# Straight-line attention code, eight input slots, and a packed last block in the feed-forward layers

## The reference

```python
h = _layernorm(x, axis=-1) * (1 + ca) + sa
x = x + ga * attn(h)        # 16 heads of 16; softmax over all 1024 keys
h = _layernorm(x, axis=-1) * (1 + cb) + sb
x = x + gb * ffn(h)         # two layers of the following
# one layer:
h = shift_token(x)          # the upper half of the columns comes from the token before
q, k, v = split(h @ wqkv)   # 8 heads of 64
q, k = rotary_xpos(l2norm(q) * qs, l2norm(k) * ksc)
x = x + local_attention(q, k, v) @ wo   # windows of 128 tokens, each with the window before it
h = layernorm(shift_token(x)) * lg + lb
a, g = split(h @ w1 + b1)   # 682 columns each
x = x + (a * gelu(g)) @ w2 + b2
```

## Time and profile before

| | us |
|---|---|
| median of three runs | 4847.93 |
| lowest, highest | 4840.43, 4849.11 |
| the profiled execution | 4837.09 |
| its span, first to last instruction | 4835.1 |

### The profile page before, as it was taken

How to read it: one execution, slowest core, us unless ns; L and a number is a source line. 1 busy time by engine, 2 the same in 40 slices (tenths; PEclk the granted TensorE clock), 3 DMA queues, 4 the chain that set the end, 5 groups by cost and what they waited for, 6 DMA issues and landing times. The chain is left out here.

```text
span 4835.1 us, 94881 instructions
## 1 busy us (share of the span) xinstructions
PE 4276.8 (88%) x27610; PEld 2744.2 (57%) x27610; DVE 3590.9 (74%) x7998; ACT 2801.1 (58%) x6209; POOL 1616.5 (33%) x2408
## 2 busy tenths in 40 slices
PE   5869999999999976599999997999799999988998
PEld 2423333333333334477777775888577777766787
DVE  6579888888888949688888784454688888875554
ACT  2438777777777850366666663333566666653333
POOL 2300000000000004455555553433455555545545
PEclk8969999999999998799999997999999999998999
DMA  6933323233233317200000002111100000012221
GB/s 204 367 54 61 60 42 60 46 57 54 48 61 50 52 63 243 72 25 26 24 24 26 24 23 63 44 54 35 49 24 25 25 24 25 25 30 85 68 65 51
DMA packets 368130, 297.05 MB, mean 61 GB/s; under 512 B 65820, under 2 KB 324888, under 8 KB 367648
## 3 DMA queue, kind: packets, MB, share of 16 engines
q1 hardware_dynamic: 367648, 291.11, 24.5%
HBM read 178.74 MB, written 111.21 MB: 60 GB/s over the span
## 5 line engine op out<-in xcount | busy, mean ns | idle before, releaser
L889 ACT ACTIVATE fa_P<-fa_pS 128x512 f32<-128x512 f32 x2048 | 1112.0, 595 | 385.7 <-PE fa_pS L815 337.6
L916 DVE TENSOR_REDUCE fa_mx<-fa_pR 128x2 f32<-128x1024 f32 x1024 | 1205.4, 1221 | 151.3 <-PE fa_pR L796 139.5
L1518 POOL TENSOR_TENSOR wa_pn<-wa_pr,wa_ri 128x512 f32<-128x512 f32 x512 | 700.7, 1369 | 614.0 <-DVE wa_ri L1574 600.4
L815 PE MATMUL fa_pS<-fa_Q,fa_K 50*128 50x512 f32 x2048 | 520.2, 504 | 108.0 <-ACT fa_P L889 77.8
L1454 ACT ACTIVATE wa_pr<-wa_sm,wa_mn 128x256 f32<-128x256 f32 x1024 | 510.4, 501 | 177.5 <-DVE wa_mn L1566 177.5
L1140 POOL TENSOR_TENSOR ao_xn<-ao_xn,ao_mod 128x1024 f32<-128x1024 f32 x16 | 37.6, 2348 | 1663.5 <-DVE ao_xn L1105 1663.5
L830 PE MATMUL fa_pO<-fa_P,fa_V 128*32 128x512 f32 x4096 | 560.1, 620 | 0.2 <-ACT fa_P L889 0.2
L815 PEld LDWEIGHTS fa_pS<-fa_Q,fa_K 50*128 50x128 f32 x2048 | 194.6, 187 | 602.9 <-ACT fa_P L889 543.4
L796 PE MATMUL fa_pR<-fa_K,fa_Q 48*128 48x512 f32 x2048 | 406.8, 451 | 60.6 <-DMA fa_K<-parts_d 38.5
L1306 PE MATMUL wa_pQK<-wa_wqkv,wa_xT 128*128 128x512 f32 x1536 | 419.7, 409 | 5.8 <-DVE wa_qa L1611 5.8
L2012 ACT ACTIVATE ff_gl<-ff_pG,ff_b 128x512 f32<-128x512 f32 x192 | 132.6, 691 | 475.2 <-PE ff_pG L1953 475.2
(11 more groups left out here) (186 smaller groups left out, 7191.8 us busy)
## 6 DMA issues: line engine op xcount, KB each, us to landing
parts_d<-pj_parts SPq DMA_DIRECT2D x64, 512.0 KB, 5.4
fa_Q<-parts_d SPq DMA_DIRECT2D x192, 128.0 KB, 4.5
fa_K<-parts_d SPq DMA_DIRECT2D x192, 128.0 KB, 6.9
v_d<-pj_v SPq DMA_DIRECT2D x16, 1024.0 KB, 8.4
fa_V<-v_d SPq DMA_DIRECT2D x32, 512.0 KB, 8.8
pj_x<-in_L_attn_x SPq DMA_DIRECT2D x16, 512.0 KB, 7.6
fa_Q<-fa_nrow SPq DMA_DIRECT2D x512, 2.0 KB
att_d<-fa_att SPq DMA_DIRECT2D x64, 128.0 KB, 2.0
```

The source lines that it names most:

```text
L815: nc.tensor.matmul(pS[:, (s * exped.per + u + e) % T, :], Ks[at:at + SROWS + 2, s, a, kb * P:(kb + 1) * P], Qs[at:at + SROWS + 2, s, a, ha ...
L889: nc.scalar.activation(Pr[:, k % 2, h, :], pS[:, (s * exped.per + u) % T, :], ACT.Exp).then_inc(exped.sem, 1)
L916: nc.vector.tensor_reduce(mx[:, q // QB, :, a, q % QB, kh], row_slot(), AX.X, ALU.max).then_inc(row_free, 1)
L1518: nc.gpsimd.tensor_tensor(pn[:, hp % 2], pr[:, hp % 2], inv, ALU.mult).then_inc(s["weighted"].sem, 1)
```

## The change

Four things are changed. Both `drive` functions of the attentions lose their loops: all 32 groups and all 67 bodies of a layer are written out on every engine, so that group and tile numbers, and the counts that waits compare with, are constants. The tiles xs and xo in local attention have eight slots (`X_BUFS`) in place of four, and SyncE loads tile n+8 after the store of tile n; the other tiles with `WIN_BUFS` slots stay at four. In feed-forward, the two halves of block 5 are packed into one block of 128 rows: the 42 value columns at rows 0 to 41, the 42 gate columns at rows 64 to 105. `up` then has eleven groups of six matmuls a tile and not twelve; gelu 5 reads rows 64 to 127 of pG, mix 5 and the splits of block 5 work on 64 rows, and mix 5 reads pG. The weights of block 5 come by one more DMA, and the unused rows of u are zeroed once. The normalization of the next tile is cut into three portions in place of five: steps 0 to 5 after mix 0, 6 to 11 after mix 1, 12 and hn after mix 2.

```diff
 WIN_BUFS = 4
+X_BUFS = NW
...
         def drive(eng, body):
-            body(0, 0)
-            loops = (GROUPS - NB) // NB
-            with eng.Fori(0, loops) as i:
-                for j in range(NB):
-                    body(i * NB + 1 + j, (1 + j) % NB)
-            for n in range(1 + loops * NB, GROUPS):
+            for n in range(GROUPS):
                 body(n, n % NB)
...
-        xs = sb("xs", [P, R, 2, P])
-        xo = sb("xo", [P, R, P])
+        xs = sb("xs", [P, X_BUFS, 2, P])
+        xo = sb("xo", [P, X_BUFS, P])
...
         def drive(eng, body):
-            for i in range(NW):
-                body(i, i)
-            with eng.Fori(1, B) as b:
-                for w in range(NW):
-                    body(b * NW + w, w)
-            for i in range(TILES, TILES + 3):
+            for i in range(TILES + 3):
                 body(i, i % NW)
...
-                for n in range(1, R):
+                for n in range(1, X_BUFS):
                     load(n, n)
-                with sp.Fori(0, TILES // R - 1) as i:
-                    for r in range(R):
-                        store(i * R + r, r % 2)
-                        load(i * R + R + r, r)
-                for n in range(TILES - R, TILES):
+                for n in range(TILES):
                     store(n, n % 2)
+                    if within(n + X_BUFS):
+                        load(n + X_BUFS, n % X_BUFS)
...
                     if within(new):
-                        turn_x(new, w % R)
+                        turn_x(new, w)
...
                     if within(end):
-                        add(end, w_end % R)
+                        add(end, w_end)
...
-        gated=HB, lifted=HB, gelu=HB, mixed=HB, u_high=HB, u_split=HB, y_done=1, summed=1, scaled=1, final=1,
+        gated=HB, lifted=HB - 1, gelu=HB, mixed=HB, u_high=HB, u_split=HB, y_done=1, summed=1, scaled=1, final=1,
...
+                w1_rows = a["L0_ffn_w1"][layer].rearrange("(k p) n -> p k n", p=P)
+                loads += [
+                    (w1_in[:, :, 0, 0:HID], w1_rows[:, :, 0:HID]),
+                    (w1_in[:, :, 1, 0:full], w1_rows[:, :, HID:HID + full]),
+                    (w1_in[:, :, 0, full + LAST:full + LAST + HL], w1_rows[:, :, HID + full:2 * HID]),
+                ]
...
+                nc.vector.memset(u[LAST:P, :, HB - 1, :].bitcast(F32), 0.0).then_inc(zeroed, 1)
...
                 def mix(n, j):
+
                     dve.wait_ge(s["gelu"].sem, s["gelu"].upto(g(n), j + 1))
-                    dve.wait_ge(s["lifted"].sem, s["lifted"].upto(g(n), j + 1))
+                    if j < HB - 1:
+                        dve.wait_ge(s["lifted"].sem, s["lifted"].upto(g(n), j + 1))
                     if not (early(n, 1) and layer == 0 and j < 2):
                         dve.wait_ge(s["u_split"].sem, g(n) * HB + j - 1)
-                    nc.vector.scalar_tensor_tensor(out=uF[:, j % 2, :], in0=pA[:, j % 2, :], scalar=b1[:, 0, j:j + 1],
-                                                   in1=gl[:, j % 2, :], op0=ALU.add,
-                                                   op1=ALU.mult).then_inc(s["mixed"].sem, 1)
+                    rows_, ps = (P, pA) if j < HB - 1 else (LAST, pG)
+                    nc.vector.scalar_tensor_tensor(out=uF[0:rows_, j % 2, :], in0=ps[0:rows_, j % 2, :],
+                                                   scalar=b1[0:rows_, 0, j:j + 1], in1=gl[0:rows_, j % 2, :],
+                                                   op0=ALU.add, op1=ALU.mult).then_inc(s["mixed"].sem, 1)
...
-                NORM_PARTS = (range(0, 1), range(1, 4), range(4, 8), range(8, 12), range(12, LN_INCS + 1))
+                NORM_PARTS = (range(0, 6), range(6, 12), range(12, LN_INCS + 1))
...
                 pe.wait_ge(w_in, 16 * LOADS)
+                pe.wait_ge(zeroed, 4)
...
                     for j in range(HB):
                         for half, ps, done, freed in ((1, pG, "gated", "gelu"), (0, pA, "lifted", "mixed")):
+                            if half == 0 and j == HB - 1:
+                                continue
                             if not (early(n, 1) and layer == 0 and j < 2):
                                 pe.wait_ge(s[freed].sem, g(n) * HB + j - 1)
+                            if half == 1 and j == 1 and not (early(n, 1) and layer == 0):
+                                pe.wait_ge(s["mixed"].sem, s["mixed"].upto(g(n - 1)))
+                            part = half if j < HB - 1 else 0
                             products = [(k, x, y) for k in range(KT) for x, y in SPLIT_PRODUCTS]
                             for i, (k, x, y) in enumerate(products):
-                                last = nc.tensor.matmul(ps[:, j % 2, :], w1[:, x, k, half, j * P:(j + 1) * P],
+                                last = nc.tensor.matmul(ps[:, j % 2, :], w1[:, x, k, part, j * P:(j + 1) * P],
...
-                    nc.scalar.activation(gl[:, j % 2, :], pG[:, j % 2, :], ACT.Gelu,
-                                         bias=b1[:, 1, j:j + 1]).then_inc(s["gelu"].sem, 1)
+                    at, rows_ = (0, P) if j < HB - 1 else (LAST, LAST)
+                    nc.scalar.activation(gl[0:rows_, j % 2, :], pG[at:at + rows_, j % 2, :], ACT.Gelu,
+                                         bias=b1[at:at + rows_, 1, j:j + 1]).then_inc(s["gelu"].sem, 1)
```

More of the change, by code:

```diff
@@ L1740, in feed_forward @@
         full = (HB - 1) * P
-        LOADS = 11
+        LOADS = 12
+        LAST = P // 2
         def g(n):
```

19 lines of the change are left out of this document (9 added, 10 removed).

## The result

| | before, us | after, us |
|---|---|---|
| median of four runs each | 4848.52 | 4623.24 |
| lowest, highest | 4840.43, 4865.0 | 4615.12, 4625.81 |
| the profiled execution's span | 4835.1 | 4613.0 |

The ratio is 0.953, with a 95% interval from 0.950 to 0.956: 225 us less. The forecast was 4626.

What follows compares the result with a forecast made beforehand. TensorE was taken as the bound, busy 1371 of 1507 us in full attention. Terms 75 + 83 + 22.4 + 35 = 215 us off 4837.1 gave 4622, 4633 with the median's 10.8; 4626 was taken, range 4595 to 4665.

Steps and rivals of the forecast that it cites:

- Full attention, 75 forecast: Full attention written out: 63 half groups at 21.67 us each take 1365 us instead of 1439.8; bounds 20 to 75.
- The 29 us of 54 halves: Full attention: 54 half groups in the loop each lose 0.54 us, with register instructions standing between the matmuls.
- The rest, the round ends: Full attention: the remainder of the 75 us is the eight loop-round ends with their slow clock.
- Local attention, 83 forecast: Local attention written out with eight slots: all tiles at 13.64 us, saving 41.8 and 40.8 us; bounds 12 to 83.
- with eight it has four bodies more, so the input waits go whatever else happens: Local attention: eight slots give each load some 55 us more, removing input waits of 6.0 us in layer 0.
- Where the instructions come from: Whole kernel: straight code's instruction fetch stays hidden, as in a written-out stretch with 5 packets; cost 0.
- The second rival: Straight code starved of instructions: 2.5 us for each of 243 packets, 608 us, time about 5230; chance 0.04.
- Feed-forward of layer 0, 22.4 forecast: Feed-forward, layer 0: one matmul group less, 1.40 us for each of 16 tiles, as TensorE never pauses; bounds 0 to 22.4.
- 3.0 us of cover: Feed-forward, layer 0: time between `split_h` ending and the next tile's matmuls; the later chain takes about 0.8 us of it.
- Feed-forward of layer 1, 35 forecast: Feed-forward, layer 1: packing and an earlier hn save 2.2 us a tile over 16 tiles; bounds 0 to 44.7.
- three steps held before mix 1: Feed-forward, layer 1: GpSimd holds small VectorE steps, mix 1 ends about 4581.6, block 3's value matmuls lose 0.6 us.
- the first rival: Feed-forward, layer 1: GpSimd always goes first, block 3 loses 1.7 us, the layer gains only 8; time 4653, chance 0.13.

Runs made afterwards that it cites:

- that experiment: Eight input slots alone against the kernel before, all loops kept: 4828.9 us, local attention 889.0 and 889.7 us a layer, no wait for an input.

## Why the prediction was right, and where it was not

**Full attention, 75 forecast, 77.3 measured: right, in size and cause.** The 29 us of 54 halves are there, but they are ScalarE's register instructions. The forecast said only that "register instructions stand between the matmuls", which put them on the wrong engine. The rest, the round ends, belongs to two engines: TensorE alone straight saves 17.2 us, ScalarE alone 38.4, both 73.9. Both together save more than the two savings add up to, since each engine's pause at a round end hides the other's.

**Local attention, 83 forecast, 92 measured: right in sum, wrong in one attribution.** The step "with eight it has four bodies more, so the input waits go whatever else happens" is true of the slots, as that experiment shows; but the forecast took it for the reason. Straight code takes them too, with four slots, where SyncE issues the load 1.1 us sooner. Of the 9 us more than forecast, 6 are tiles of 13.59 us in place of 13.64 (2 x 63 x 0.05). The other 3 come from the last two tiles of layer 1, which took 23.6 us before as well and which the forecast had counted as full tiles. With straight code, four slots and eight are alike. I had read a wait of at most 1.1 us as a matter of distance in tiles, and not looked at what SyncE does between the addition and the load.

**Where the instructions come from: right.** 193 packets, no pause for issue on TensorE in full attention (445 to 1650 us) and none over 0.3 us in local attention. The second rival needed 0.9 us a packet. The Trainium skill (Runtime: NRT & Kernel Launch, "Instruction fetch mechanics") says that a taken branch whose target lies outside the prefetched instructions forces a fetch, while straight code streams. The traces agree: waits of up to 3.8 us at the ends of long rounds, and none over 0.3 us in straight code.

**Feed-forward of layer 0, 22.4 forecast, 23.6 measured: right in size, wrong in reason.** The step that fails is "TensorE has no pause in this stage, so 22.4 us go, if nothing else is late". I looked for what becomes late at the tile's end and gave it 3.0 us of cover; hn, ready just in time before the transposes, I credited to layer 1 alone. By the packing alone the layer gains 1.7 us in all. The three portions, which I had put at nothing in this layer, make the gain possible, and give 0.17 us a tile of their own. The forecast counted 16 tiles and the distances are 15: 15 x 1.40 = 21.0, and 2.6 of the portions, are the 23.6. (One row less stands ahead of the transposes than before, the six value matmuls of block 5, and not two as the remark above the order of instructions says.)

**Feed-forward of layer 1, 35 forecast, 27.4 measured: the mechanism is right, the term too large.** The wait moved from hn to mix 1 as described. The forecast had three steps held before mix 1 and 0.6 us lost at block 3; four were held and 1.39 lost, nearer to the first rival's 1.7 than to 0.6. The fourth is L86, whose two inputs both lie in SBUF. The Trainium skill (SBUF — State Buffer, "Who interferes with whom") says that this form contends with GpSimd's reads, and the rows at 4403.52 and 4395.04 agree: 1.19 and 1.14 us behind the start of a GpSimd operation, 0.16 without. Its rule of the lock gave 8 us for a VectorE that loses every race, and that didn't happen: held steps and GpSimd's operations took turns, one for one. That the additions of GpSimd are the cause is shown: with them behind the splits, the wait and 22 us are gone. A part of the 27.4 is luck: the kernel before had two falls of the clock in this stage and the changed one none. Against unchanged code without a fall (417.0 us, in the kernel with TensorE's code straight) the gain is 24.1.

**The range** of 4595 to 4665 held the result. The errors of the terms were +2.3, +9.0, +1.2 and -7.6 us; they cancel in part, to +4.9, and the hit of the sum, 3 us, is better than its terms deserve.

## What to carry to other kernels

- Where an engine loop's round is long, write it out or shorten the round, and do so on every engine of the pipeline at once: in full attention each engine's pause at the round end hid the other's, and one engine's straight code gave a quarter (TensorE) or a half (ScalarE) of the gain of both.
- Less work on the busiest engine is worth nothing if its next operand is only just in time. Read the time between the operand's end and its use in the timeline before you credit the saving, and move the producer with it.
- Before a transfer is given more buffers, look at what its issuing engine does between the event that frees the buffer and the issue. And put GpSimd operations that nobody waits for behind those that somebody waits for, since each of them can also hold a small VectorE step.

## What the runs showed of the hardware

- A round end cost TensorE 2.5 us on the mean in full attention (20.1 / 8) and 3.6 in local attention (21.4 / 6), ScalarE 1.8 and 2.5 (14.1 / 8, 14.8 / 6), and TensorE 1.6 and 2.0 with six feed-forward tiles a round. With two such tiles a round there was none.
- After most pauses of TensorE at round ends in the attentions the granted clock went to 1.2 GHz for 3.4 to 13.7 us, but after those in feed-forward it didn't. In feed-forward of layer 1, with the same waits for hn (22 us), the clock fell not at all in one kernel, twice in another and six times in a third, and the layer took 417.0, 420.2 and 426.6 us. With waits of 41.4 us it fell 11 times. What decides is open.
- In the loop ScalarE's gap before each step of full attention was 0.42 us, in straight code 0.34; 0.08 for eight steps is 0.64, near the 0.54 that a half group lost.
- A VectorE step on 128x4 of the normalization takes 0.15 to 0.17 us alone. If it starts while a GpSimd operation runs, it ends with it, 0.02 to 0.03 us later: it takes 1.14 to 1.35 us behind the start of one of 1.26 to 1.30 or where that much was left of one of 2.41, and 0.3 to 0.8 where less was left. If it starts first, even by 0.04 us, it takes its 0.16 (an L84 in each of 15 tiles a layer). The memset of the same tile took 0.06 us beside a GpSimd operation.
